# Four products of a query/key pair accumulate onto each other in PSUM, and ScalarE keeps the running sums

## The reference, cut to what matters

```python
qkv = x @ w_qkv.T
q = q * cos + _rotate_half(q) * sin          # the same for k
scores = where(0 <= pos_q - pos_k < 64, q @ k.T * scale, -inf)
x = _layernorm(x + (softmax(scores) @ v) @ w_out.T)
x = _layernorm(x + ((silu(x @ w_gate * s_gate) * (x @ w_up * s_up)) @ w_down) * s_down)
```

## Time and profile before

| | |
|---|---|
| median of three runs | 1167.48 us |
| span of the profiled execution | 1164.2 us |
| TensorE busy | 1154.0 us, 99% |
| VectorE, ScalarE, GpSimd busy | 984.6, 584.4, 587.3 us |
| one turn of the loop (228 to 370 us, and the like) | 141.9 us |

### The profile page before, as it was taken

The page is one execution under the profiler, slowest core; times in us unless marked ns, Lnnn a source line. Parts: engine busy times, 40 slices in busy tenths (PEclk is TensorE's granted clock), DMA queues, the critical chain, the costliest instruction groups (busy, mean ns, idle before and its releaser), DMA issues.

```text
span 1164.2 us, 25539 instructions
## 1 busy us (share of the span) xinstructions
PE 1154.0 (99%) x8433; PEld 567.9 (49%) x8433; DVE 984.6 (85%) x2821; ACT 584.4 (50%) x1640; POOL 587.3 (50%) x563
## 2 busy tenths in 40 slices
PE   9999999999999999999999999999999999999998
PEld 4344446444464444644455444554445444464444
DVE  7899998898987899879998899897898988986434
ACT  3953883048820588105880169701686027950330
POOL 0775684156731667326771367613676236752330
PEclk9999999999999999999999999999999999999999
DMA  9999786366562765617656096561964537734000
GB/s 295 173 175 252 137 166 160 66 88 137 111 149 55 110 131 107 145 41 128 132 97 141 37 146 119 101 132 46 155 123 88 131 63 137 120 73 109 19 2 36
DMA packets 352077, 134.80 MB, mean 116 GB/s; under 512 B 309840, under 2 KB 332496, under 8 KB 351952
## 3 DMA queue, kind: packets, MB, share of 16 engines
q1 hardware_dynamic: 334976, 106.86, 49.6%
q0 software_dynamic: 10560, 17.30, 5.1%
q10 hardware_dynamic: 6416, 9.00, 2.1%
HBM read 32.19 MB, written 8.39 MB: 35 GB/s over the span
## 4 chain that ended last, share of the span: by engine, by line
PE 97%; DVE 1%; ACT 1%; issue 1%; POOL 0%; POOLq 0%; DVEq 0%
PE bank L842 61%; PE bank L1058 18%; PE bank L848 10%; PE bank L984 3%; PE bank L964 2%; PE bank L864 1%; PE bank L1080 1%; ACT bank L1243 1%; PE bank L873 0%; PE bank L1069 0%; PE bank L948 0%; DVE wd L1373 0%; ACT wu L1186 0%; DVE ffn_tmp L1530 0%; ACT fuse L1186 0%
## 5 line engine op out<-in xcount | busy, mean ns | idle before, releaser
L842 PE MATMUL bank<-x1T,wg 128*128 128x512 f16 (+1 forms) x1032 | 242.5, 378 | 0.0
L842 PE MATMUL bank<-x1T,wu 128*128 128x512 f16 x1024 | 241.9, 379 | 0.0
L1243 ACT ACTIVATE bank<-bank,neg_max,qk_scale 128x128 f32<-128x128 f32 x512 | 220.5, 435 | 7.8 <-DVE neg_max L1558 6.1
L1058 PE MATMUL bank<-wd,fuse 128*128 128x512 f16 (+2 forms) x1056 | 222.7, 373 | 0.0
L660 POOL TENSOR_TENSOR fuse<-ffn_tmp,fuse 128x512 f16<-128x512 f32 x128 | 149.7, 1170 | 117.5 <-ACT fuse L1186 116.8
L742 POOL TENSOR_TENSOR fuse<-fuse 128x512 f16<-128x512 f32 x116 | 137.7, 1218 | 74.9 <-ACT fuse L1186 72.8
L1058 PEld LDWEIGHTS bank<-wd,fuse 128*128 128x128 f16 x1056 | 101.9, 98 | 118.0
L842 PEld LDWEIGHTS bank<-x1T,wu 128*128 128x128 f16 x1024 | 100.1, 98 | 120.7
L655 POOL TENSOR_TENSOR xT_sb<-probs,xT_sb 128x512 f16<-128x512 f32 x112 | 129.6, 1158 | 44.5 <-ACT xT_sb L1186 44.4
L842 PEld LDWEIGHTS bank<-x1T,wg 128*128 128x128 f16 x1032 | 96.3, 98 | 113.9 <-issue 4.0
L1196 ACT ACTIVATE ffn_tmp<-bank,tanh_scale 128x512 f32<-128x512 f32 x128 | 88.2, 689 | 100.0 <-PE bank L842 76.8
(11 more groups left out here) (235 smaller groups left out, 1621.5 us busy)
## 6 DMA issues: line engine op xcount, KB each, us to landing
v_cross<-v_own SPq DMA_DIRECT2D x64, 128.0 KB, 2.4
out<-x ACTq DMA_DIRECT2D x31, 256.0 KB, 2.0
xT_sb<-xT SPq DMA_DIRECT2D x30, 256.0 KB, 4.1
qkT<-x SPq DMA_DIRECT2D x28, 256.0 KB, 3.8
wg<-w_gate POOLq DMA_DIRECT2D x7, 1024.0 KB, 5.2
wu<-w_up POOLq DMA_DIRECT2D x7, 512.0 KB, 6.0
wqkv<-w_qkvT SPq DMA_DIRECT2D x8, 256.0 KB, 6.3
wg<-w_gate POOLq DMA_DIRECT2D x1, 2048.0 KB, 8.4
```

What stands on the lines that cost most here:

```text
L842: last = pe.matmul(dst, lhsT, rhs, start=(i == 0), stop=(i == len(pairs) - 1))
L1058: last = pe.matmul(dst[:, cols], fuse[:, s, z, rows], wd[:, s, cols], start=(s == 0 and z == 0), stop=(s == STEPS - 1 and z == 1))
L1243: last = act.activation(unit, unit, ACT.Exp, bias=neg_max[:, s % 2, h // 3, h % 3:h % 3 + 1], scale=qk_scale[:, 2:3], accum_out=row_sum[:, ...
```

## The change

Five of the seven products now share two banks. First, sixth, seventh and fourth go one after the other onto the bank of back even, without clearing it; fifth and third go onto front odd; second goes to front even. Before the next product is added, ScalarE copies what stands in the bank to SBUF: after the first, fifth, sixth and seventh (`keep_first`, `keep_fifth`, `keep_sixth`, `keep_seventh`; event `products_kept`, 8 a tile). VectorE adds three times a pair: front even += first, back odd = kept fifth + kept seventh (both in SBUF, result in the bank), front odd += kept sixth. Back even needs no addition. `x_sums` and `w_sums` change places to fit, and TensorE waits for the copies ahead of sixth, seventh, third and fourth. In the loop the order of products becomes first, fifth, sixth, second, seventh, third, fourth. At the end of `first()` it becomes second, `weigh_v(15)`, first, `project_o(3)`, fifth, sixth, third, seventh, fourth, and `project_v(0)` moves behind them. The diff, without renamed places and without the bodies of functions taken out:

```diff
-        first_kept = ev("first_kept", 2)
-        pair_summed = ev("pair_summed", 14)
+        products_kept = ev("products_kept", 8)
+        pair_summed = ev("pair_summed", 6)
...
+            return rope_other if i == 0 else [rows[:, n, :] for rows in (y, ffn_tmp) for n in range(2)]
...
-                sum_second_x()
+                sum_first_x(1)
+                pool.sem_inc(x_summed[0], 4)
...
-            def product(dst, pairs):
+            def product(dst, pairs, onto=False):
                 for i, (lhsT, rhs) in enumerate(pairs):
-                    last = pe.matmul(dst, lhsT, rhs, start=(i == 0), stop=(i == len(pairs) - 1))
+                    last = pe.matmul(dst, lhsT, rhs, start=(i == 0 and not onto), stop=(i == len(pairs) - 1),
+                                     skip_group_check=onto)
                 return last
+
+            def quarter(dst, lhsT, rhs, onto=False):
+                return product(dst, [(lhsT[:, k, :], rhs[:, k, :]) for k in range(KC // 2)], onto)
...
-            def project_pair(a, i, first=False):
-                front_even, front_odd, back_even, back_odd = pair_banks(i)
+            def pair_first(a, i):
                 front_low, front_high, back_low, back_high = x_quarters(i)
                 low_even, odd_less_even, high_even, high_odd = w_quarters()
-                sums, turn = x_sums(i), turn_of(i)
...
+                done(first_product, quarter(pair_banks(i)[2], front_low, low_even))
+
+            def pair_second(a, i):
+                front_low, front_high, back_low, back_high = x_quarters(i)
+                low_even, odd_less_even, high_even, high_odd = w_quarters()
+                done(second_product, quarter(pair_banks(i)[0], front_high, high_even))
+
+            def pair_fifth(a, i):
+                low_even, odd_less_even, high_even, high_odd = w_quarters()
+                pe.wait_ge(w_summed, 4)
+                done(fifth_product, quarter(pair_banks(i)[1], x_sums(i)[:, 1, :, :], odd_less_even))
+
+            def pair_sixth(a, i):
+                wait(products_kept, pe, a - 1, 4 * turn_of(i))
+                done(sixth_product, quarter(pair_banks(i)[2], x_sums(i)[:, 2, :, :], w_sums[:, 1, :, :], True))
+
+            def pair_seventh(a, i):
+                wait(products_kept, pe, a - 1, 4 * turn_of(i) + 2)
+                done(seventh_product, quarter(pair_banks(i)[2], x_sums(i)[:, 0, :, :], w_sums[:, 2, :, :], True))
+
+            def pair_third(a, i):
+                low_even, odd_less_even, high_even, high_odd = w_quarters()
+                wait(products_kept, pe, a - 1, 4 * turn_of(i) + 1)
+                done(qk_done, quarter(pair_banks(i)[1], x_sums(i)[:, 3, :, :], high_odd, True))
+
+            def pair_fourth(a, i):
+                front_low, front_high, back_low, back_high = x_quarters(i)
+                wait(products_kept, pe, a - 1, 4 * turn_of(i) + 3)
+                done(qk_done, quarter(pair_banks(i)[2], back_high, w_sums[:, 0, :, :], True))
+
+            def project_pair(a, i):
                 for j in (2 * i, 2 * i + 1):
                     wait_xT(pe, a, j)
...
+                wait(*((proj_read, pe, a - 1, NB - 1) if i == 0 else (down_read, pe, a - 2, NB - 1)))
+                pair_first(a, i)
+                wait(x_summed, pe, a - 1, 7)
+                pair_fifth(a, i)
+                pair_sixth(a, i)
+                pair_second(a, i)
+                pair_seventh(a, i)
+                pair_third(a, i)
+                pair_fourth(a, i)
...
-                        project_v(a + 1, 0, True)
-                project_pair(a + 1, 1, True)
+                        for j in range(2, NB):
+                            wait_xT(pe, a + 1, j)
+                        wait(proj_read, pe, a, 1)
+                        pair_second(a + 1, 1)
+                wait(proj_read, pe, a, 2)
+                pair_first(a + 1, 1)
+                project_o(a, NB - 1, ffn)
+                wait(x_summed, pe, a, 3)
+                pe.wait_ge(w_summed, 3)
+                pair_fifth(a + 1, 1)
+                pair_sixth(a + 1, 1)
+                pair_third(a + 1, 1)
+                pair_seventh(a + 1, 1)
+                pair_fourth(a + 1, 1)
+                project_v(a + 1, 0, True)
...
             def keep_first(a, i):
                 wait(first_product, act, a - 1, turn_of(i))
-                if i:
-                    wait(ln2_chain, act, a - 2, 4 * 2)
-                done(first_kept, copy(kept_products(i)[0], pair_banks(i)[0]))
+                done(products_kept, copy(kept_products(i)[0], pair_banks(i)[2]))
+
+            def keep_fifth(a, i):
+                wait(fifth_product, act, a - 1, turn_of(i))
+                done(products_kept, copy(kept_products(i)[1], pair_banks(i)[1]))
+
+            def keep_sixth(a, i):
+                wait(sixth_product, act, a - 1, turn_of(i))
+                done(products_kept, copy(kept_products(i)[2], pair_banks(i)[2]))
+
+            def keep_seventh(a, i):
+                wait(seventh_product, act, a - 1, turn_of(i))
+                done(products_kept, copy(kept_products(i)[3], pair_banks(i)[2]))
 
...
                 split_high(a + 1, 0, True)
+                keep_first(a + 1, 1)
                 for j in range(2):
                     split_x1_high(a, j, ffn)
                 split_high(a + 1, 1, True)
-                keep_first(a + 1, 1)
+                keep_fifth(a + 1, 1)
+                keep_sixth(a + 1, 1)
+                keep_seventh(a + 1, 1)
                 carry_v(a + 1)
                 for j in range(2, NB):
...
                 for j in range(NB):
                     if more and j == 2:
                         keep_first(a + 1, 0)
+                    if more and j == 3:
+                        keep_fifth(a + 1, 0)
+                        keep_sixth(a + 1, 0)
                     wait(y_ready, act, f, j)
                     cols = STORED_HALVES[1] if not attn and j == NB - 1 else slice(0, EMB)
                     dst = out[bass.ds(f * TILE + j * P, P), cols]
                     act.dma_start(dst, x1[:, j, cols]).then_inc(y_moved[j], 16)
                 if more:
+                    keep_seventh(a + 1, 0)
                     keep_first(a + 1, 1)
                     split_high(a + 1, 0, ffn)
+                    keep_fifth(a + 1, 1)
+                    keep_sixth(a + 1, 1)
+                    split_high(a + 1, 1, ffn)
+                    keep_seventh(a + 1, 1)
                     carry_v(a + 1)
-                    split_high(a + 1, 1, ffn)
...
-            def sum_front_even(a, i):
+            def add_front_even(a, i):
                 front_even = pair_banks(i)[0]
+                wait(products_kept, dve, a - 1, 4 * turn_of(i))
                 wait(second_product, dve, a - 1, turn_of(i))
                 done(pair_summed, dve.tensor_tensor(front_even, front_even, kept_products(i)[0], ALU.add))
 
-            def sum_front_odd(a, i):
+            def add_back_odd(a, i):
+                wait(products_kept, dve, a - 1, 4 * turn_of(i) + 3)
+                done(pair_summed, dve.tensor_tensor(pair_banks(i)[3], kept_products(i)[1], kept_products(i)[3], ALU.add))
+
+            def add_front_odd(a, i):
                 front_odd = pair_banks(i)[1]
                 wait(qk_done, dve, a, 2 * i)
                 done(pair_summed, dve.tensor_tensor(front_odd, front_odd, kept_products(i)[2], ALU.add))
 
...
             def rope_front(a, i):
-                sum_front_even(a, i)
-                wait(pair_summed, dve, a - 1, 7 * turn_of(i) + 4)
+                add_front_even(a, i)
+                wait(pair_summed, dve, a - 1, 3 * turn_of(i))
                 rope_products(a, 2 * i, True, range(2), paired=True)
-                sum_front_odd(a, i)
-                if i:
-                    sum_back_even(a, i)
-                wait(pair_summed, dve, a - 1, 7 * turn_of(i) + 5)
+                add_back_odd(a, i)
+                add_front_odd(a, i)
+                wait(pair_summed, dve, a - 1, 3 * turn_of(i) + 2)
                 rope_products(a, 2 * i, True, range(2, 4), paired=True)
                 rope_sums(a, 2 * i, True)
-                if i == 0:
-                    sum_back_even(a, i)
 
             def rope_back(a, i):
-                wait(pair_summed, dve, a - 1, 7 * turn_of(i) + 6)
+                wait(qk_done, dve, a, 2 * i + 1)
                 rope_products(a, 2 * i + 1, True, paired=True)
...
                 take_x1(a, 3, ffn)
                 start_x1(a, 3, ffn)
-                sum_second(a + 1, 1)
                 split_x1(a, 2, ffn)
-                sum_fourth(a + 1, 1)
                 finish_x1(a, 3, ffn)
-                sum_back_odd(a + 1, 1)
                 split_x1(a, 3, ffn)
                 rope_front(a + 1, 1)
...
-                    sum_second(a + 1, 0)
-                    sum_fourth(a + 1, 0)
                     carry_keys(a + 1)
                     start_tables(a + 1)
                 finish_y(f, NB - 1)
```

(33 more changed lines are left out.)

21 lines of the change are left out of this document (6 added, 15 removed).

## The result

The changed kernel takes 1171.16 us (median of 5 runs, 1170.57 to 1172.20), the kernel before 1167.15 (5 runs, 1165.75 to 1167.51, of which three are those of the table ahead of the prediction): ratio 1.0036, 95% interval 1.0023 to 1.0048. The forecast was 1171.0. That the two times agree to 0.2 us is in part luck: the loss came out 0.5 larger than forecast, and the median of the kernel before 0.3 lower. The span went from 1164.2 to 1168.9 us, of which 0.6 lies ahead of everything that was changed (the first `weigh_v(14)` row starts at 90.38 in place of 89.78).

The account below looks back on a forecast made before the run. TensorE was taken to bound the kernel. VectorE's 3.54 us at the end of `first()`, containing TensorE's own 2.17, plus 0 for the loop gave 1167.5 + 3.5 = 1171.0 us, range 1168.2 to 1174.2.

Parts of the forecast that it names:

- TensorE bounds all of it: Whole kernel: TensorE is full in the loop, so VectorE's 31 us of saved additions is worth nothing directly.
- TensorE's holes in first(): End of `first()`: TensorE loses 0.94, 0.09, 0.1 and 1.04 us ahead of first, `project_o(3)`, third and fourth; sum 2.17.
- VectorE's queue: End of `first()`: seventh's copy delays `split_x1_high(2)`, so `split_x1(2)` starts 4.25 us late; after gains and losses, 3.54 us.
- The 0.55: End of `first()`: extra time for `add_back_odd`, reading two SBUF tiles while GpSimd runs `split_low(1)`; +0.55 us.
- VectorE's part on top of TensorE's own: End of `first()`: VectorE's 3.54 us goes straight to TensorE and contains TensorE's own 2.17.
- The edge to TensorE closed already: Second gate product: already waits for `split_v(3)`, ending 124.44 against weights loading at 124.49, so VectorE's 3.54 us reaches TensorE.
- The loop: Six turns: seventh's copy behind `split_high(1)` fits with 0.3 us to spare; 0 lost, at most 0.5 us a turn.
- Faster: Rival: gaps before the second gate product are VectorE waits; earlier VectorE saves up to 2.1 us, 1165.4; chance 0.05.
- The signs: Timeline: TensorE holes about 0.9 and 1.0 us, VectorE idle some 5 us, `split_v(0)` near 121.7, turn 141.9.
- The total: Whole kernel: span 1164.2 + 3.5 = 1167.7 us, median 1171.0 us, +0.3%; chance of 3 to 4.5 us is 0.5.

Follow-up runs that it names:

- e4: Against the changed kernel, the edits of e2 and e3 together, both at the end of `first()`: 1167.76 us, ratio to before 1.0006.
- e8: e4 against the changed kernel, plus, in the loop, the seventh's copy of pair 1 moved ahead of `split_high(1)`: 1167.17 us, ratio to before 1.0002.
- e2: Against the changed kernel, ScalarE's `split_x1_high(2)` and `(3)` moved ahead of the sixth's and seventh's copies in `first()`: 1169.91 us, ratio to before 1.0025.
- e3: Against the changed kernel, `project_v(0)` in `first()` cut in two halves, placed ahead of the first and fourth products: 1171.97 us, ratio to before 1.0044.

## Why the prediction was right, point by point

- **TensorE bounds all of it.** Right. VectorE's freed time is worth nothing: e4 has 52 additions fewer and VectorE 26 us less busy (31 was forecast, counted from start to start), and its rest is still 0.4 above before, which its turns of 142.00 us explain. In e8 nothing is lost either, but there only 14.6 us are freed, so e4 is the cleaner test.
- **TensorE's holes in first(), forecast 0.94, 0.09, 0.10, 1.04, sum 2.17.** Measured 1.83: `project_v(1)` starts at 108.64 + 3.43 = 112.07, less 0.60, against 109.64. It is 0.50 ahead of first, nothing ahead of `project_o(3)`, 0.27 and 0.85 ahead of third and fourth, and 0.10 each for the rows of these two (1.98 us in place of 1.88). The step that was off is the adding up, by 0.33, and not the start times: fourth at 106.33 puts `project_v(1)` at 106.33 + 1.72 + 3.43 = 111.48, 1.84 late. The sum counts the first hole from 92.15, but the earlier trace rows give 94.08 - 3.43 + 1.72 = 92.37 (92.36 measured), and the 0.09 ahead of `project_o(3)` is in the kernel before as well (1.83 from first's start to its own, 1.82 after). That the start of third came true (101.83 for 101.85) is luck: fifth's copy ended 0.18 later than forecast, as `split_high(1)` was no sooner than before, and third started 0.05 after it and not 0.25.
- **VectorE's queue, forecast 4.25 - 1.93 - 0.23 + 0.78 + 0.12 + 0.55 = 3.54.** `split_v(0)` came at 122.47 - 0.60 = 121.87, 3.68 late. Start of `split_x1(2)`: 107.75, forecast 107.65. From there 14.12 us, forecast 14.08. That this agrees so well is luck in one term. The 0.55 was meant for `add_back_odd`, which beside GpSimd's `split_low(1)` lost 0.16 (0.85 against 0.69), from start to start 0.07. `split_x1(3)`, for which nothing was counted, lost 0.51 (1.19 against 0.68). GpSimd's row here, and `split_x1(3)` in the kernel before, where it lost nothing beside the same work of GpSimd:

```profile
109.68 5.41 POOL L741 TENSOR_TENSOR fuse<-fuse 128x512 f16<-128x512 f32 x4 [5.92 <-DVE x L1624]
```

```profile
106.39 0.68 DVE L1605 SCALAR_TENSOR_TENSOR qkT<-x,qkT 128x512 f16<-128x512 f32 x1
```

What decides is where the other engine's current instruction stands. One subtraction of GpSimd takes 1.16 us when it doesn't wait. The first of these four runs from 109.68 to 110.84, `split_x1(3)` started in its midst at 110.20 and ended 0.55 us after it; the third runs from 112.37 to 113.53, `add_back_odd` started near its end, at 113.24, and again ended 0.56 after it. In the kernel before `split_x1(3)` started 0.09 before a subtraction ended, and there GpSimd paid: its next one took 1.64 us. That whichever of the two starts first holds the shared ports for its whole instruction, and the other waits for its end, is what the Trainium skill says (SBUF — State Buffer, section SBUF: two separate sides), and the trace agrees.
- **VectorE's part on top of TensorE's own.** Forecast 3.54 - 2.17 = 1.37, measured 1.9 (by e2). The total of the stretch agreed because it goes by VectorE's path, which was sized right, and not by the sum of holes.
- **The edge to TensorE closed already.** Right: `split_v(3)` ended 128.73 and the product started 128.78, the same 0.05 as before, and 3.69 of stretch stands against VectorE's 3.68.
- **The loop, forecast 0 with 0.3 us of room, at most 0.5 a turn.** Here 0.07 a turn, at the place named: small, but 0.5 us in all and a turn of 142.00 where 141.9 was to stay. The step that was off is the end of `rope_sums(1)`. Its two sums were put at 1.23 and 1.64 and took 1.68 and 1.64, so that seventh's copy started 0.5 us later than forecast (534.03 less 4.43, by which the pairs start later than in the earlier trace rows, makes 529.60, against 529.1). Timeline of VectorE, changed kernel:

```profile
528.66 1.68 DVE L1428 TENSOR_TENSOR fuse<-fuse 128x512 f32<-128x512 f32 x1
530.26 1.64 DVE L1429 TENSOR_TENSOR fuse<-fuse 128x512 f32<-128x512 f32 x1
```

- **Faster, by gaps ahead of scores and gate products.** Wrong as a rival. In the turn of the earlier trace rows, from the start of the plain projections to VectorE's `split_v(0)` it is 541.53 - 531.98 = 9.55 us in the kernel before and 542.64 - 536.48 = 6.16 in the changed one, so VectorE is 3.4 us earlier; to the second gate product it is 18.22 us in both (550.20 - 531.98 and 554.70 - 536.48). So those gaps are no waits for VectorE.
- **The signs.** The holes were named after block 2's addition and a ScalarE copy, as foretold, but of 0.50 and 0.85 us with the profile's own waits at 0.42 and 0.69, where 0.9 and 1.0 had been said; VectorE idled 5.22 us and `split_v(0)` came at 121.87, against 121.7.
- **The total.** 3.5 forecast, 4.0 measured between the medians (1.5 either way by the interval), 3.7 + 0.5 = 4.2 by the parts of the trace.

## What to carry to other kernels

Work taken off an engine that doesn't set the end is worth nothing, but the waits put in its place can cost: look at what stands in the queues behind each new wait, and who needs it. When a copy has to wait for a product, put what is ready ahead of it; and when two causes hold the same edge, closing one may show nothing or a loss until the other is gone, so test them together as well as alone.

## What was not expected of the hardware

An addition with both inputs in SBUF writing to PSUM took 0.70 us with GpSimd quiet, as those that read a bank do, and 0.85 and 1.08 beside GpSimd's subtractions. The f16 split on VectorE, 0.69 in the earlier trace rows, took 1.19 in e2, e3, e4 and the changed kernel, where a subtraction of GpSimd had started 0.5 us before, and 0.68 in the kernel before, where one was about to end. So an order that frees VectorE can give part of it back by what it then runs beside: e8 and e4 do the same work, and VectorE is 12 us busier in e8.

Adding onto a bank that ScalarE has just read costs TensorE nothing: 14 products take 24.03 us in e8, where eight of them accumulate onto what was read, as in the earlier trace rows, where none does.
